# One-hot comparisons for eight steps at a time instead of four in the adjacency build of a graph network on Trainium2

## The reference

```python
edge_index = jnp.stack([src, dst])
x = _layernorm(x + _L0_gnn_ref(x, edge_index, ...))   # 4 x: agg = segment_sum(x[src], dst) * inv_deg; h = agg @ Wl.T + bl + x @ Wr.T; norm; relu
x = _layernorm(x + _L1_gnn_ref(x, edge_index, edge_weight, ...))
x = _layernorm(x + _L2_gnn_ref(x, src, dst, ...))     # attention over edges, feed-forward
x = _layernorm(x + _L3_gnn_ref(x, edge_index, ...))
```

## Time and profile before

| | |
|---|---|
| Median of 3 runs | 1564.66 us (1561.86 to 1576.53) |
| The profiled execution, its own time | 1565.19 us |
| Its span, first to last instruction | 1563.4 us |
| TensorE busy / weight loads busy | 1184.6 us (76%) / 880.4 us (56%) |
| VectorE / ScalarE / GpSimd busy | 783.1 (50%) / 437.5 (28%) / 411.2 us (26%) |
| Adjacency build, first comparison to last copy | about 54 to 199.5 us of the span |
| Line 644 (matmuls of the steps), 625 times | 100.6 us busy, its loads 84.5 us |
| Lines 574 and 576 (comparisons), 157 times each | 65.2 us busy for line 574 |
| Line 683 (copies to `counts`), 157 times | 91.1 us busy |

### The profile page before, as it was taken

How to read it: one execution, slowest core, us unless ns; L and a number is a source line. 1 busy time by engine, 2 the same in 40 slices (tenths; PEclk the granted TensorE clock), 3 DMA queues, 4 the chain that set the end, 5 groups by cost and what they waited for, 6 DMA issues and landing times. The chain is left out here.

```text
span 1563.4 us, 21486 instructions
## 1 busy us (share of the span) xinstructions
PE 1184.6 (76%) x7694; PEld 880.4 (56%) x7694; DVE 783.1 (50%) x1938; ACT 437.5 (28%) x869; POOL 411.2 (26%) x490
## 2 busy tenths in 40 slices
PE   2599989999999979444767676847776655777795
PEld 1477745555555635444656676746666655775453
DVE  4877737544455655513544444544454534455333
ACT  0566612111111111321323232322333323334111
POOL 3000000000000000116555555555555564520000
PEclk9977799999999999676878787878888878888998
DMA  5000060000000000133222222222222222218000
GB/s 144 12 1 1 1 209 0 8 0 8 1 1 20 21 12 1 30 119 106 82 78 80 85 82 73 83 75 80 80 71 81 73 86 71 81 48 181 24 20 22
DMA packets 49633, 87.99 MB, mean 56 GB/s; under 512 B 12261, under 2 KB 35320, under 8 KB 49291
## 3 DMA queue, kind: packets, MB, share of 16 engines
q0 software_dynamic: 20608, 55.20, 12.2%
q1 hardware_dynamic: 26442, 29.96, 7.0%
q10 hardware_dynamic: 2492, 1.61, 0.4%
HBM read 70.74 MB, written 15.98 MB: 55 GB/s over the span
## 5 line engine op out<-in xcount | busy, mean ns | idle before, releaser
L1303 POOL DMA_INDIRECT counts_all<-kv_d,counts_all x416 | 393.5, 946 | 342.1 <-DVE counts_all L1367 175.2
L812 PE MATMUL bank<-counts_all,parts 125*128 (+2 forms) x2100 | 410.6, 354 | 27.2 <-DVE parts L983 9.7
L1418 PE MATMUL bank<-counts_all 125*128 125x128 f32 x1384 | 225.5, 327 | 189.2 <-ACT counts_all L1461 158.6
L1418 PEld LDWEIGHTS bank<-counts_all 125*128 125x128 f32 x1384 | 207.8, 236 | 205.0 <-ACT counts_all L1461 171.1
L812 PEld LDWEIGHTS bank<-counts_all,parts 125*128 125x128 f16 x2100 | 191.4, 97 | 231.1 <-issue 17.5
L1429 PE MATMUL bank<-counts_all,oh 128*125 128x136 f32 x1384 | 210.4, 299 | 31.8 <-issue 28.2
L1429 PEld LDWEIGHTS bank<-counts_all,oh 128*125 128x125 f32 x1384 | 187.2, 203 | 37.8 <-issue 35.0
L1367 DVE TENSOR_TENSOR counts_all<-counts_all,bank 128x512 f32<-128x512 f32 x104 | 71.2, 685 | 226.8 <-ACT counts_all L1487 173.0
L1461 ACT CAST counts_all<-bank 125x1024 f32<-125x1024 f16 (+1 forms) x104 | 90.0, 865 | 290.1 <-remote 173.5
L1194 POOL IOTA iota_n<- 128x250 f16 x1 | 0.3, 346 | 584.6 <-POOLq L796 584.6
L1469 ACT CAST oh<-parts 128x1000 f32<-128x1000 f16 (+1 forms) x104 | 92.2, 886 | 187.8 <-remote 156.0
(11 more groups left out here) (211 smaller groups left out, 1105.1 us busy)
## 6 DMA issues: line engine op xcount, KB each, us to landing
counts_d<-counts_all SPq DMA_DIRECT2D x1, 6835.9 KB
counts_all<-kv_d,counts_all POOLq DMA_INDIRECT x416
counts_all<-counts_d SPq DMA_DIRECT2D x1, 6152.3 KB
kv_d<-counts_all SPq DMA_DIRECT2D x6, 500.0 KB
q_d<-counts_all SPq DMA_DIRECT2D x1, 1562.5 KB
x<-in_x SPq DMA_DIRECT2D x6, 250.0 KB
out<-z SPq DMA_DIRECT2D x6, 250.0 KB
inv_deg<-in_x SPq DMA_DIRECT2D x1, 1400.0 KB
```

What stands on the lines that cost most here:

```text
L812: last = T.matmul(agg_ps[p][:, 0:w], pin[:, s, part, :], counts[:, s, bass.ds(b * BLK, w)], start=(s + part == 0), stop=(s + part == NT))
L1303: G.indirect_dma_start(out=out_rows, out_offset=None, in_=table_d, in_offset=bass.IndirectOffsetOnAxis(ap=index, axis=0)).then_inc(signal, 16)
L1418: last = T.matmul(ps[2 + n % 2][:, k * C:(k + 1) * C], ohT[n % 2][:, w, k, :], Q[:, GTILES[n][w], :], start=(w == 0), stop=(w == nw - 1))
```

## The change

A batch is now eight steps. The comparisons write [128, 125, 8], 1000 elements each, so the 125 numbers of one step lie 8 elements, 16 bytes, apart. There are 79 batches: 78 of eight steps and one of one. The matmuls of a batch go to two banks, four steps (HALF) to each, so three batches (SLOTS) take banks 0 to 5, and the sums of the degrees move to banks 6 and 7. ScalarE still copies four steps at a time. `batch_done` and `batch_out` now count halves, and the function `outs(n)` gives how many halves there are in the first n batches: VectorE waits for both halves of the batch three before, and TensorE waits for both copies of the batch three before. `x_low` stands after the third batch instead of the fourth. The degree blocks come two batches of eight after their last window instead of three of four. `oh_sl` is a tile of its own in place of a part of `parts1`. The tables `iota_kp` and `iota_tp` have twice the elements.

```diff
--- before.py
+++ after.py
@@ -31,9 +31,11 @@
 WKEYS = WN * NT
 WCODES = WN * N
 WBLK = NW // TILE
-BATCH = 4
+BATCH = 8
+HALF = 4
 NBATCH = -(-NW // BATCH)
 OHR = 3
+SLOTS = 3
 MAGIC = 12582912.0
 FAR = 16777216.0
 GWN = 25
@@ -167,7 +169,6 @@
         kcol = carve_early([LANES, NW], fp16)
         slcol = carve_early([LANES, NW], fp16)
         oh_key = [carve_early([LANES, WKEYS, BATCH], fp16) for _ in range(OHR)]
-        oh_sl = [carve_early([LANES, TILE, BATCH], fp16) for _ in range(OHR)]
         iota_kp = carve_early([LANES, WKEYS, BATCH], fp16)
         iota_tp = carve_early([LANES, TILE, BATCH], fp16)
         early_general = early_at[0]
@@ -489,6 +490,7 @@
         with s2:
             t = lambda name, shape, dt: sb(name, shape, dt, s2)
             ones_h = t("ones_h", [TILE, 128], fp16)
+            oh_sl = [t(f"oh_sl{i}", [LANES, TILE, BATCH], fp16) for i in range(OHR)]
 
             keyN = t("keyN", [LANES, CHP], fp32)
             slN = t("slN", [LANES, CHP], fp32)
@@ -530,13 +532,25 @@
             def in_batch(n):
                 return min(BATCH, NW - n * BATCH)
 
-            PER_BLK = BLK // (BATCH * WN)
-            DEG_LAG = 3
+            DEG_LAG = 2
+
+            def last_batch(b):
+                return ((b + 1) * BLK - 1) // (BATCH * WN) if b < NBLK else NBATCH - 1
 
             def degree_blocks_after(n):
 
-                return [b for b in range(NBLK + 1) if min(b * PER_BLK + PER_BLK - 1 + DEG_LAG, NBATCH - 1) == n
-                        or (b == NBLK and n == NBATCH - 1)]
+                return [b for b in range(NBLK + 1) if min(last_batch(b) + DEG_LAG, NBATCH - 1) == n]
+
+            def halves(n):
+
+                return [(h, min(HALF, in_batch(n) - h * HALF)) for h in range(2) if in_batch(n) > h * HALF]
+
+            def batch_bank(n, h):
+                return ps[2 * (n % SLOTS) + h]
+
+            def outs(n):
+
+                return sum(len(halves(m)) for m in range(n))
 
             def degree_width(b):
                 return min(BLK, N - b * BLK)
@@ -569,13 +583,13 @@
                     with dve.If(general <= 0):
                         for n in range(NBATCH):
                             if n >= OHR:
-                                dve.wait_ge(batch_done, n - OHR + 1)
+                                dve.wait_ge(batch_done, outs(n - OHR + 1))
                             k, cols, slot = in_batch(n), slice(n * BATCH, n * BATCH + in_batch(n)), n % OHR
                             V.tensor_tensor(oh_key[slot][:, :, 0:k], iota_kp[:, :, 0:k],
                                             kcol[:, cols].unsqueeze(1).to_broadcast([LANES, WKEYS, k]), ALU.is_equal)
                             V.tensor_tensor(oh_sl[slot][:, :, 0:k], iota_tp[:, :, 0:k],
                                             slcol[:, cols].unsqueeze(1).to_broadcast([LANES, TILE, k]), ALU.is_equal).then_inc(oh_ready, 1)
-                            if n == OHR:
+                            if n == 2:
                                 x_low()
                     with dve.Else():
                         x_low()
@@ -612,7 +626,7 @@
                             pe.wait_ge(deg_copied, b - 1)
                         w = degree_width(b)
                         for s in range(NT):
-                            last = T.matmul(ps[4 + b % 2][:, 0:w], ones_h[:, :], counts[:, s, b * BLK:b * BLK + w],
+                            last = T.matmul(ps[6 + b % 2][:, 0:w], ones_h[:, :], counts[:, s, b * BLK:b * BLK + w],
                                             start=(s == 0), stop=(s == NT - 1))
                         last.then_inc(deg_done, 1)
 
@@ -638,14 +652,15 @@
                     with pe.If(general <= 0):
                         for n in range(NBATCH):
                             pe.wait_ge(oh_ready, n + 1)
-                            if n >= 4:
-                                pe.wait_ge(batch_out, n - 3)
-                            for i in range(in_batch(n)):
-                                last = T.matmul(ps[n % 4][0:TILE, i * WKEYS:(i + 1) * WKEYS], oh_sl[n % OHR][:, :, i],
-                                                oh_key[n % OHR][:, :, i], start=True, stop=True)
-                            last.then_inc(batch_done, 1)
+                            if n >= SLOTS:
+                                pe.wait_ge(batch_out, outs(n - SLOTS + 1))
+                            for h, k in halves(n):
+                                for i in range(k):
+                                    last = T.matmul(batch_bank(n, h)[0:TILE, i * WKEYS:(i + 1) * WKEYS], oh_sl[n % OHR][:, :, h * HALF + i],
+                                                    oh_key[n % OHR][:, :, h * HALF + i], start=True, stop=True)
+                                last.then_inc(batch_done, 1)
                             for b in degree_blocks_after(n):
-                                pe.wait_ge(batch_out, min((b + 1) * PER_BLK, NBATCH))
+                                pe.wait_ge(batch_out, outs(last_batch(b) + 1))
                                 degrees(b)
                     with pe.Else():
                         pe.sem_inc(pair_free, BK)
@@ -666,7 +681,7 @@
                         act.wait_ge(x_low_ready, 1)
                         act.wait_ge(deg_done, b + 1)
                         w = degree_width(b)
-                        S.copy(inv_deg[:, b * BLK:b * BLK + w], ps[4 + b % 2][:, 0:w]).then_inc(deg_copied, 1)
+                        S.copy(inv_deg[:, b * BLK:b * BLK + w], ps[6 + b % 2][:, 0:w]).then_inc(deg_copied, 1)
 
                     def evacuate(w, slot):
                         a, b = banks(slot)
@@ -678,10 +693,12 @@
                     general = not_all_hit(ET.Activation)
                     with act.If(general <= 0):
                         for n in range(NBATCH):
-                            act.wait_ge(batch_done, n + 1)
-                            k, at0 = in_batch(n), n * BATCH * WN
-                            S.copy(counts[:, :, at0:at0 + k * WN].rearrange("p s (w d) -> p s w d", d=WN),
-                                   ps[n % 4][0:TILE, 0:k * WKEYS].rearrange("p (w s d) -> p s w d", s=NT, d=WN)).then_inc(batch_out, 1)
+                            for h, k in halves(n):
+                                act.wait_ge(batch_done, outs(n) + h + 1)
+                                at0 = (n * BATCH + h * HALF) * WN
+                                S.copy(counts[:, :, at0:at0 + k * WN].rearrange("p s (w d) -> p s w d", d=WN),
+                                       batch_bank(n, h)[0:TILE, 0:k * WKEYS].rearrange("p (w s d) -> p s w d", s=NT, d=WN)
+                                       ).then_inc(batch_out, 1)
                             for b in degree_blocks_after(n - 1):
                                 take_degrees(b)
                         for b in degree_blocks_after(NBATCH - 1):
```

## The result

The changed kernel is slower by 2.9%: 1613.29 us (1612.07 to 1616.01, 4 runs) against 1568.19 us for the kernel before (1561.86 to 1576.53, 4 runs), ratio 1.029, 95% interval 1.026 to 1.032. The prediction was 1611 us. The medians lie 45.1 us apart.

What follows compares the result with a forecast made beforehand. VectorE at 0.164 us a step and degree blocks by turns bound the build. At 0.235 us a step, 55.5 + 146.9 + 1.4 + 38.6 + 1.2 + 1.6 ends it at 245.2, 46.1 us later: 1611 us; range 1550 to 1618.

Steps and rivals of the forecast that it cites:

- What bounds the kernel now: Adjacency build: VectorE at 0.164 us a step and the degree blocks by turns; TensorE's own pace 0.118, limited by SBUF reading.
- The comparisons: VectorE in the build: 1000 elements take 690 ns, 0.60 us start to start; 9.0 us of work goes.
- The pace at 16 bytes: TensorE's step matmuls: 0.235 us a step, in proportion to the memory passed over; bounds 0.118 to 0.235.
- The straight line through 0.057 and 0.118: TensorE's step pace from reads over 250 and 1000 bytes, giving 0.198 us at 2000 bytes; judged too flat.
- The degree blocks: TensorE in the build: six blocks take 38.6 us, 6.44 each, as before; the last block 1.6 us.
- the upper end of the range: Whole kernel: 1618 us, with 0.235 us a step and all degree blocks as long as the longest, 7.17 us.
- The sum: End of the build: TensorE's terms add to 245.2 us against 199.1 now, 46.1 us more, giving 1611.3 us.
- the 0.100 us of neighbours at the lower clock: TensorE's loads at line 1407: starts (0.93 - 0.23) / 7 = 0.100 us apart at clock 0.50.
- The rest: ScalarE's copies stay 0.115 us a step, GpSimd's tables grow to some 5 us under idle time, later layers unchanged.
- Rival 1: Step matmuls: the step in memory costs nothing, the saving comes through; 13 us go, 1552 us, 0.8% faster; chance 0.26.
- Its stops: VectorE at degree blocks: six stops fall from 5.7 to 5.0 us each, saving 4.1 us, if TensorE's pace stays 0.118.
- The two rules weighed there: TensorE reads: 16-byte lines need two hits, though 8 bf16 are free; loads take columns / 1.2, 104 ns for 125.

Runs made afterwards that it cites:

- groups of four: Changed kernel with one-hots laid out [lanes, 2, 125, 4], 8 bytes from number to number: 1377.74 us against 1395.35 for the kernel before; again 1557.30 against 1570.47.
- the ring of four: Changed kernel with steps grouped by four (8 bytes from number to number) and OHR = 4 buffers, not three: 1546.19 us against 1568.17 for the kernel before.
- at 4 bytes: Changed kernel with one-hots laid out [lanes, 4, 125, 2], 4 bytes from number to number: 1549.65 us against 1568.17 for the kernel before.
- at 32 bytes: Kernel before, batches of four, both operands 32 bytes from number to number, two ring buffers in place of three: 1646.60 us against 1568.17.

## Why the prediction was right

*What bounds the kernel now.* Right: TensorE alone would do a step in 0.118 us and was near to being the bound; its reading, not its clock, set that pace. The runs confirm the reading of it: it holds in all five traces of kernels that read both operands with 8 bytes (the kernel before, the one with `oh_sl` moved, groups of four twice, the ring of four), and falls to 0.060 at 4 bytes.

*The comparisons.* 690 ns and 0.60 us apart were forecast; 681 ns and 0.59 us came (54.12, 54.72, 55.31 in VectorE's timeline).

*The pace at 16 bytes.* 0.235 was forecast, 0.229 came: 625 x 0.006 = 3.8 us too much. The value was taken from the right end of the bounds, but the reason given for it, that the stretch of memory passed over is what costs, is wrong: at 32 bytes it costs the same. That the number came out so near is luck in this part. The price is per line, and 8 to 16 bytes doubles the lines as it doubles the distance. The straight line through 0.057 and 0.118, which gave 0.198 and the lower end of the forecast's own range, was too flat for the reason named: at 4 bytes the pace is still the array's.

*The degree blocks.* 38.6 us for six were taken over unchanged. They took 41.6 (6.32, 7.52, 7.22, 6.30, 6.60 and 7.66 us, from start to the next step), and the last, small one 2.25 in place of 1.56. That is 3.7 us too little, and it makes up for the 3.8 too much. More of each block runs at the lower level of the clock. The second block of each kernel starts at 99.77 before and at 112.92 now and has a mean granted clock of 0.89 and 0.70 (length, busy, clock, DMA, GB/s):

```profile
99.77:105.70 5.93, 5.93 (x25) 0.89 0.01 3
```

```profile
112.92:120.44 7.52, 7.52 (x25) 0.70 0.00 0
```

Over the five blocks that have a record of it the mean is 0.84 before (0.75 to 0.91) and 0.75 now (0.68 to 0.84). In both kernels TensorE enters these blocks at 1.2 GHz and the clock rises within them, at 101.1 us before and at 117.5 us now in the two shown, so 1.3 and 4.6 us after their start; why it rises later isn't shown. The prediction named this effect, but only as the upper end of the range. The step matmuls themselves don't mind: 0.92 us of the changed kernel hold all or part of five loads at either level, and in all its loads the median from start to start is 0.229 us at both:

```profile
122.00:122.92 0.92, 0.92 (x5) 1.00 0.00 0
130.00:130.92 0.92, 0.92 (x5) 0.50 0.00 0
```

*The sum.* 55.5 + 146.9 + 1.4 + 38.6 + 1.2 + 1.6 = 245.2 was forecast for the end of the build. The trace has 55.45 + 143.1 + 1.5 + 41.6 + 1.3 + 2.25 = 245.2, and 245.36 is where it ends. Two terms missed by nearly 4 us with opposite signs; the end is nearer than the working deserves.

*Two numbers in the working.* The upper end of the range, 1618, is 2 us over what its two terms give (1611.3 and 6 x 0.73 = 4.4, so 1615.7). And the 0.100 us of neighbours at the lower clock is too short, since the second load of such a group starts at once: at 4 bytes, where the array sets the pace too, the starts lie 0.107 us apart at 1.2 GHz. Neither changes the forecast.

*The rest* (ScalarE, GpSimd's tables, the layers after) was to stay, and did: 1364.3 and 1364.8 us behind the build.

*Rival 1* was wrong in its condition: the distance does cost. Its price can be checked all the same, since groups of four steps make its condition true. It forecast 13 us less; the two measurements are 17.6 us (of 1395) and 13.2 us (of 1570), with the build 15.1 and 15.9 us shorter. Its stops were 5.0 us each as worked out, but five and not six: when the last degree block comes, all batches of the kernel are already made.

*The two rules weighed there.* By the note on cachelines of the Trainium skill (page SBUF — State Buffer, section Door 1: The DMA port swizzle) a line has 16 bytes and needs two hits for full speed. The traces agree on the line; not on the two hits, which cost 0.118 us where four cost 0.060; nor on a distance of 8 bf16 being free, which costs 0.229 here with fp16, a type of the same size. By the Trainium skill's rule for loads (page TensorE: Matmul & The Clock Gate, section LDWEIGHTS) a load's time is its columns divided by 1.2, an estimate of 104 ns for 125, and nothing in it depends on the distance. The traces come near that only at 4 bytes and 1.2 GHz (0.107 us from start to start); they have 0.060 at 2.4 GHz, and 0.229 at 16 bytes.

## What to carry to other kernels

When elements of several steps are interleaved so that one VectorE instruction can make them all, the interleaving sets how far apart TensorE finds the numbers of one operand, and TensorE pays for each 16-byte line that it touches. Count the lines of each operand, multiply the larger count by the 1.83 ns of these runs, and compare that with the pace of the engine that bounds now; before a batch is made larger, group its steps so that the distance stays at 8 bytes, or at 4, which costs the comparison nothing (675 and 672 ns). A spare buffer ahead of a periodic stall is worth a try beside the cheaper instruction: here it took 9.5 us off the build, part of it by a higher clock, where the larger batches had taken off 15.1.

## What the runs showed of the hardware that was not expected

- Reading an operand of 125 fp16 numbers costs TensorE 1.83 to 1.88 ns per new 16-byte line, at either level of its clock. The stationary and the moving operand are read side by side at nearly the same price (0.227 us a step with only the weights 16 bytes apart, 0.224 with only the moving operand, 0.229 with both). At 8 bytes a step already takes twice the 0.060 us of 4 bytes.
- A VectorE comparison of 1000 fp16 elements keeps its 0.67 to 0.68 us when its second input has runs of eight, four or two numbers (681, 675 and 672 ns).
- With a fourth buffer in the ring the granted clock in the build was 0.98 in place of 0.89, and a degree block took 5.3 to 5.4 us in five of six cases, where it had taken 5.4 to 6.9. Why is open.
- The same kernel before took 1395 us beside one group of runs and about 1570 beside the others, and the build is as long in both: with groups of four it ended at 184.0 us in the one and at 183.2 in the other. The cause is open.
